# Second router of a two-layer MetaFormer kernel: logits of four token tiles in four column groups of TensorE

## The reference, cut to what matters

```python
x = x + spectral_mixer(_ln_c(x), ...)                 # layer 0
t = t + moe0(_ln_t(t), router_w, gate_w, up_w, down_w)
x = x + criss_cross_attention(_ln_c(x), ...)          # layer 1: 3x3 convolution, attention down and along, two gates
t = t + moe1(_ln_t(t), w_router, w1_stack, w2_stack, ws1, ws2)
```

```python
x = hidden_tensor.reshape(-1, Cc)            # 4096 x 256, normalised
logits = x @ w_router.T                      # 4096 x 8
probs = jax.nn.softmax(logits, axis=-1)
expert_weight, expert_idx = jax.lax.top_k(probs, TOP_K)    # 2 of 8 experts for each token
```

## Time and profile before

| | us |
|---|---|
| median of 3 runs | 1138.05 (1137.79 to 1139.34) |
| span of the profiled execution | 1136.6 |
| TensorE busy in it | 995.8 (88%) |
| VectorE, ScalarE, GpSimd busy | 615.9 (54%), 530.4 (47%), 267.8 (24%) |
| router matmuls L1351 busy, both ends modelled | 25.0 in the second half of the attention stage |

### The profile page before, as it was taken

The page is one execution under the profiler, slowest core; times in us unless marked ns, Lnnn a source line. Parts: engine busy times, 40 slices in busy tenths (PEclk is TensorE's granted clock), DMA queues, the critical chain, the costliest instruction groups (busy, mean ns, idle before and its releaser), DMA issues. The chain is left out here.

```text
span 1136.6 us, 19741 instructions
## 1 busy us (share of the span) xinstructions
PE 995.8 (88%) x5614; PEld 807.2 (71%) x5614; DVE 615.9 (54%) x1713; ACT 530.4 (47%) x1344; POOL 267.8 (24%) x274
## 2 busy tenths in 40 slices
PE   6866579999999999993688999999884799998999
PEld 1743368888888888882466666776543699997998
DVE  6887643332332232224756577555778455554776
ACT  6536444443444444433243443433324466666774
POOL 0000021111111111104752200000000344442776
PEclk9558659999999999996789999999655599999999
DMA  9544411111111111205532201101140244443554
GB/s 382 237 149 148 149 32 52 52 52 56 52 52 56 55 52 53 57 29 172 182 120 84 66 28 57 38 19 75 65 139 19 92 139 141 136 137 117 171 182 144
DMA packets 63235, 114.68 MB, mean 101 GB/s; under 512 B 9698, under 2 KB 43124, under 8 KB 62132
## 3 DMA queue, kind: packets, MB, share of 16 engines
q1 hardware_dynamic: 49908, 77.72, 19.3%
q0 software_dynamic: 12960, 35.41, 11.0%
q10 hardware_dynamic: 288, 0.47, 0.1%
HBM read 73.96 MB, written 39.59 MB: 100 GB/s over the span
## 5 line engine op out<-in xcount | busy, mean ns | idle before, releaser
L600 POOL DMA_INDIRECT experts_rows_sb<-h_rows,choices x142 | 134.3, 946 | 731.3 <-POOLq L428 401.8
L795 DVE TENSOR_TENSOR experts_a_sb<-experts_a_sb,experts_bankU 128x512 f32<-128x512 f32 x71 | 48.9, 689 | 225.3 <-PE experts_bankU L183 225.3
L746 ACT ACTIVATE experts_a_sb<-experts_bankG 128x512 f32<-128x512 f32 (+1 forms) x142 | 69.7, 491 | 92.7 <-PE experts_bankG L183 92.6
L737 ACT ACTIVATE experts_hT<-experts_bankH 128x256 fp32r<-128x256 f32 x142 | 54.3, 382 | 90.5 <-PE experts_bankH L663 90.2
L759 ACT ACTIVATE experts_y_sb<-experts_bankY 128x256 f32<-128x256 f32 x142 | 54.7, 385 | 87.6 <-PE experts_bankY L180 66.8
L1182 POOL DMA_INDIRECT attn_y<-y_rows,choices x64 | 65.7, 1027 | 92.4 <-POOLq L120 38.1
L181 PE MATMUL attn_bankC<-attn_padded,attn_w_high 128*128 128x512 f32 x144 | 68.0, 472 | 16.7 <-ACT attn_feat L1468 14.0
L916 POOL DMA_INDIRECT shared_y<-y_rows,choices x64 | 67.5, 1055 | 38.5 <-POOLq L555 19.3
L180 PE MATMUL experts_bankY<-down_plain,experts_aT_plain 128*128 x284 | 72.9, 379 | 0.0
L186 DVE TENSOR_TENSOR experts_aT<-experts_bankA,experts_aT 128x256 fp32r<-128x256 f32 x142 | 59.7, 420 | 23.0 <-ACT experts_aT L754 23.0
L670 PE MATMUL experts_bankA<-konst_sb,experts_a_sb 128*128 128x128 f32 x426 | 70.0, 273 | 1.7 <-DVE experts_aT L186 1.7
(11 more groups left out here) (370 smaller groups left out, 2752.7 us busy)
## 6 DMA issues: line engine op xcount, KB each, us to landing
y_rows<-experts_y_sb SPq DMA_DIRECT2D x142, 128.0 KB, 1.7
h_rows<-xn SPq DMA_DIRECT2D x32, 256.0 KB, 2.1
mix_xT<-in_xt SPq DMA_DIRECT2D x4, 1024.0 KB, 12.3
x_res<-in_x SPq DMA_DIRECT2D x4, 1024.0 KB, 14.1
gate_raw<-in_L_ffn_gate_w SPq DMA_DIRECT2D x2, 2048.0 KB, 13.0
up_raw<-in_L_ffn_up_w SPq DMA_DIRECT2D x1, 4096.0 KB, 24.9
x_rows<-x_res SPq DMA_DIRECT2D x16, 256.0 KB
x_res<-x_rows SPq DMA_DIRECT2D x8, 512.0 KB, 4.8
```

The lines of the kernel that those rows point to most:

```text
L600: nc.gpsimd.indirect_dma_start(rows[t % DEPTH][:, :], None, h_dram, bass.IndirectOffsetOnAxis(ap=ids_i[:, t:t + 1], axis=0)).then_inc(s_ro ...
L746: nc.scalar.activation(a_sb[i % RING][:, :], bankG[i % RING][:, 0:hidden], ACT.Silu if gate is not None else ACT.Relu).then_inc(s["act"], 1)
L795: nc.vector.tensor_tensor(a_sb[i % RING][:, :], a_sb[i % RING][:, :], bankU[i % RING][:, 0:hidden], ALU.mult).then_inc(s["a"], 1)
```

## The change

The logits of one pair are now made by four matmuls of 128 tokens (one tile each) for each half of the channels. Tile t writes the 32 output partitions 32t to 32t+31, all at columns 0 to 127 of `bankX`. The stationary operand is padded from 8 to 32 columns with zeros, so that every partition is written. `route` is called once, in the third place, and waits for both halves of `xT`. One ScalarE copy of 128 x 128 and one 128 x 128 transpose then bring tokens back to partitions, and VectorE picks 8 of each 32 columns.

```diff
+ROUTE_M = 32
-            logits_t = sb("moe1_logits_t", [E, 512], on=on)
+            logits_t = sb("moe1_logits_t", [P, P], on=on)
-                def route(p, n, kc):
-                    pe.wait_ge(s["f_copied"], p * 2 + n + 1)
+                def route(p):
+                    pe.wait_ge(s["f_copied"], p * 2 + 2)
                     pe.wait_ge(s["feat2"], min(p + 3, PAIRS))
                     if p:
                         pe.wait_ge(s["f_kept"], p)
-                    part = slice(n * 256, (n + 1) * 256)
-                    last = nc.tensor.matmul(bankX[0:E, part], router1[:, kc * E:(kc + 1) * E], xT[:, kc * 512 + n * 256:kc * 512 + (n + 1) * 256],
-                                            start=(kc == 0), stop=(kc == KC - 1))
-                    if (n, kc) == (1, KC - 1):
-                        last.then_inc(s["f_logits"], 1)
+                    for kc in range(KC):
+                        for t in range(PT):
+                            last = nc.tensor.matmul(bankX[t * ROUTE_M:(t + 1) * ROUTE_M, 0:P], router1[:, kc * ROUTE_M:(kc + 1) * ROUTE_M],
+                                                    xT[:, kc * 512 + t * P:kc * 512 + (t + 1) * P], start=(kc == 0), stop=(kc == KC - 1))
+                    last.then_inc(s["f_logits"], 1)
 
                 def turn_logits(p):
                     pe.wait_ge(s["f_logits_t"], p + 1)
-                    for t in range(PT):
-                        last = nc.tensor.transpose(bankX[:, t * E:(t + 1) * E], logits_t[:, t * P:(t + 1) * P], K("ident", E)[:, 0:E])
-                    last.then_inc(s["f_turned_back"], 1)
+                    nc.tensor.transpose(bankX[:, 0:P], logits_t[:, :], K("ident")).then_inc(s["f_turned_back"], 1)
...
                     convolve(i, 6, 8)
                     turn(i + 1, 0)
-                    route(i - 5, 0, 0)
                     gate_layer(i - 2, 3)
                     scores(i - 1, "along")
                     convolve(i, 8, 10)
-                    route(i - 5, 0, 1)
-                    route(i - 5, 1, 0)
                     gate_layer(i - 2, 4)
                     convolve(i, 10, 12)
-                    route(i - 5, 1, 1)
+                    route(i - 5)
                     branch(i)
                     gate_layer(i - 2, 5)
...
-                    nc.scalar.activation(logits_t[:, :], bankX[0:E, :], ACT.Copy).then_inc(s["f_logits_t"], 1)
+                    nc.scalar.activation(logits_t[:, :], bankX[:, 0:P], ACT.Copy).then_inc(s["f_logits_t"], 1)
...
-                    last = nc.vector.tensor_copy(logits1[:, p * PT * E:(p + 1) * PT * E], bankX[:, 0:PT * E])
+                    last = nc.vector.tensor_copy(logits1[:, p * PT * E:(p + 1) * PT * E].rearrange("p (t e) -> p t e", e=E),
+                                                 bankX[:, 0:P].rearrange("p (t m) -> p t m", m=ROUTE_M)[:, :, 0:E])
...
-        router1 = sb("router1_sb", [P, KC * E])
+        router1 = sb("router1_sb", [P, KC * ROUTE_M])
...
-        "L1_ffn_w_router": by_contracted_row(a["L1_ffn_w_router"][None]),
+        "L1_ffn_w_router": by_contracted_row(np.pad(a["L1_ffn_w_router"], ((0, ROUTE_M - E), (0, 0)))[None]),
```

## The result

The changed kernel takes 1125.08 us (median of 5 runs, 1123.99 to 1125.71); the kernel before, on the same chip, 1137.79 us (5 runs, 1135.37 to 1139.34). The ratio is 0.9896 with a 95% interval of 0.9877 to 0.9915, which is 9.7 to 14.0 us, 11.8 in the middle; the two medians are 12.7 us apart. The forecast was 1127.3 us in a range of 1124 to 1135, 10.75 us gained. The span of the profiled execution is 1123.0 us, that of the kernel before 1136.6.

A forecast was written before the change was run, and what follows sets the result against it. TensorE was taken to bound full-clock iterations 5 to 7, chains of short waits the later ones. Savings of 4.35 + 1.9 + 1.0 + 0.9 + 3.0 = 11.15 us, less 0.4, gave 1127.3 us, range 1124 to 1135.

The forecast's parts named there:

- The value of T: Length of the merged `route` block on TensorE: 0.6 us at the full clock, 1.1 us at 1.2 GHz.
- the analogy from row groups in the mixer to column groups: Mixer's inverse showed two row-group streams 0.04 us apart; column groups assumed to overlap likewise, four at once, chance 0.58.
- the serial rival: One stream: column groups don't overlap, block 3.6 us (1.96 at full clock), 2.9 us slower, 1141 us; chance 0.13.
- Iterations 5 to 7: Full-clock attention iterations, TensorE full: merged matmuls and transposes save 1.45 us in each of three, 4.35 us together.
- The small discount on the transposes: Iterations 5 to 7: four transposes become one; only 0.05 of 0.2 us credited, as `turn_gated` would wait for VectorE.
- about 25.5 us: Sign to look for: iteration 6 should take this long and still be full, against a stretch of 27.00 us.
- Iteration 8: Gate layer 5 comes over 2 us sooner, then the softmax chain binds: 1.9 us saved, between 0.95 and 2.4.
- Iteration 9: Gate layers 3 and 4 no longer wait for `route`; layer 5 starts at 817.75 instead of 818.72: 1.0 us.
- Iterations 10 to 12: Iteration 10 repeats iteration 9, 0.9 us; at the stage's end the last `keep_logits` comes 3.0 us sooner.
- The turn through VectorE: Iteration 9, time from gate layer 3 to layer 4 through VectorE: at most 1.14 us.
- the 0.1 us for a change of tiles: Iteration 9: 0.1 us added to the `route` block of 1.1 us before layer 5.
- The 0.4 us taken off for the clock: Deducted from the 11.15 us sum: less-busy TensorE in iterations 8 to 10 may get the full clock later.

The follow-up runs named there:

- experiment 1: The changed kernel with the same eight matmuls all in the first column group, copy of 32 x 512 and four transposes: 1141.6 us, ratio 1.0041 to the kernel before.
- experiment 8: The changed kernel with the first router also in two column groups, its logits turned back by two matmuls with identity columns: 1130.57 us, ratio 0.9936.
- experiment 10: The changed kernel with the first router also in two column groups, its logits turned back by one 64 x 128 transpose: 1125.24 us, ratio 0.9874.
- experiment 5: The changed kernel run again unchanged, as yardstick for other runs: 1126.59 us, ratio 0.9888 to the kernel before.
- experiment 4: The changed kernel with the two loops of `route` swapped, both channel halves of one tile before the next tile: 1128.64 us, ratio 0.9914.
- experiment 3: The kernel before with its four unpacked `route` calls all moved to the third place, old copy and transposes: 1138.78 us, ratio 1.0014.
- experiment 11: The changed kernel with idle float32 matmuls added on TensorE in iterations 8 to 12 to hold the clock up: 1126.83 us, ratio 0.9891.

## Why the prediction was right

*The value of T, which decided everything.* Forecast 0.6 us at the full clock and 1.1 at 1.2 GHz; measured 0.57 to 0.58 and 1.01. The step was the analogy from row groups in the mixer to column groups, and it carried. That it would was a guess with one row behind it. The rule of the Trainium skill that the prediction set against it ("TensorE: Matmul & The Clock Gate", Part 3: weight loads overlap with matmuls in flight only when their row group differs) does not hold here: all four tiles use all rows, and the sixteen loads of the block in iteration 5 were over at 707.24, while its matmuls held TensorE until 707.44.

```profile
706.86 0.38 PEld L1354 LDWEIGHTS attn_bankX<-moe_xT,router_sb 128*32 128x32 f32 x16 [0.41 <-issue]
```

The prediction was wrong to take this rule for the serial rival. In the one column group of experiment 1 the loads of iteration 5 lie beside the matmuls as well, 1.67 us within a block of 1.86, with starts of records 0.11 us apart:

```profile
708.43 1.67 PEld L1354 LDWEIGHTS attn_bankX<-moe_xT,router_sb 128*32 128x32 f32 x16 [0.41 <-issue]
```

So loads that wait are not what makes one group slow; there the matmuls stream one after another, and in four groups side by side. The other page of the Trainium skill, "TensorEngine Tiling (Array Packing)", gives in its overview up to four times for 32 columns; the traces of experiment 1 and of the new kernel have 1.86 / 0.58 = 3.2 at the full clock and 3.55 / 1.01 = 3.5 at 1.2 GHz.

*Iterations 5 to 7*: forecast 4.35 us, measured 1.43 + 1.36 + 1.40 = 4.2. The small discount on the transposes was right: in iteration 5 `turn_gated` now waits 0.18 us for VectorE, where the earlier trace rows had work. One sign was misread: "about 25.5 us" for iteration 6 takes the stretch of 27.00 us in the earlier trace rows for the iteration. The iteration took 30.63 us and now takes 29.27; the 1.36 between them is what was meant.

*Iteration 8*: forecast 1.9, measured 3.1 and 2.1 (2.5 as the mean of five). The mechanism was right, for the softmax does bind now: `turn_probs` waits 0.39 us for it, in both profiles. What goes beyond the cap of 1.9 goes with the clock, which I had kept as it was. In the first profile and in experiments 8 and 10 the first scores ran wholly or nearly at the full clock, 0.98 to 1.06 us for eight records, and the iteration took 23.96 to 24.40 us, 2.6 to 3.1 less than before. In experiments 5 and 4 they took 1.68 and 1.78 us, longer than the 1.26 of the kernel before, and the iteration 25.01 and 25.10, 1.9 to 2.0 less. Nothing here shows what decides between the two; what exceeds the cap is luck. The timeline of TensorE in iteration 8, of the kernel before (where `route` follows at 791.84), of the new one and of experiment 5:

```profile
790.58 1.33 PE L1250 MATMUL attn_bankS_down<-attn_q_down 16*128 16x128 f32 x8
```

```profile
785.22 1.05 PE L1251 MATMUL attn_bankS_down<-attn_q_down 16*128 16x128 f32 x8
786.20 0.30 PE L1290 MATMUL attn_bankG<-attn_hidden,gates_wh 64*64 64x32 f32 x2
```

```profile
785.65 1.75 PE L1251 MATMUL attn_bankS_down<-attn_q_down 16*128 16x128 f32 x8
787.33 0.42 PE L1290 MATMUL attn_bankG<-attn_hidden,gates_wh 64*64 64x32 f32 x2
```

*Iteration 9*: forecast 1.0, measured 0.6 and 1.6, mean 1.0. *Iterations 10 to 12*: forecast 0.9 + 3.0, measured 5.0 and 4.0, mean 4.2. The new copy takes 0.28 us, not 0.37: line 1514, my model for it, is an exponential and not a plain copy. The turn through VectorE is 0.92 us, not up to 1.14. Both are small and on my side. So is the 0.1 us for a change of tiles: the step from layer 4 to `route` is 0.35 us (807.95 to 808.30), as the one from layer 3 (at 815.43) to the second place in the kernel before.

*The 0.4 us taken off for the clock* was in part called for. Iteration 9 of the first profile ran wholly at 0.50 (0.62 before) and gained least of all five; its iteration 10 had 0.80 between layers 0 and 5, 5.72 us, where experiment 5 with the same work had 0.50 and 6.67. So the clock gave as well as took. With the means of the five profiles the stage gains 11.9 us, 0.8 better than the sum without the discount; what is left of the 12.7 us between the medians lies outside the stage.

*The chance of 0.13 for one stream* was a fair price for an analogy; experiment 1 shows that, had it failed, the change would have been slower, as the sum said. What the shorter copy and the single transpose bring was not tried by itself.

## What to carry to other kernels

Small float32 products with few output rows, done tile by tile into the four groups of 32 output partitions, cost somewhat under a third of the same columns in one stream (0.58 of 1.86 us), the padding of the stationary operand included; the copy and the turning back become one each as well. Count first whether TensorE is what the stage waits for: it paid here because its iterations were full or because the product stood inside a chain. A merge into one place takes away the overlap that the separate calls had with waits, and the moved kernel of experiment 3 was no faster; the merge needs the shorter block to pay.

## What the runs showed of the hardware that was not expected

A column group takes several matmuls ahead while others start: four records in a row to the same group cost 0.02 to 0.03 us in all. Each block of packed matmuls costs some 0.15 us on top of its streaming (0.36 us for half a block, 0.57 for a whole one), so two half blocks are worse than one whole. Most of that isn't due to packing: the unpacked blocks of two, four and eight records took 0.53, 0.96 and 1.82 us (experiment 3), by the same working some 0.1 each.

The granted clock doesn't follow busy TensorE in any simple way. In experiment 11 it stayed at 0.50 through 9 us in which TensorE was busy throughout. A profile of the new kernel differs from the next by 1.05 us in iterations 8 and 9, in opposite directions, while two of the kernel before agree within 0.1 us. Before the router even starts, iteration 3 took 30.38 us in one profile of the new kernel and 31.89 in the other; its first 10 us had a clock of 0.86 in the one and 0.69 in the other. Such a step of 1.5 us lies outside the change and is as large as the gain of one iteration.
